# A first cross-attention that turns one unit of sixteen through TensorE, with small jobs moved off VectorE

## What is computed

```python
def _fq_unsigned(x, axis):
    s = jnp.max(x, axis=axis, keepdims=True) / 255.0
    s = jnp.maximum(s, 1e-08)
    q = jnp.clip(jnp.round(x / s), 0.0, 255.0) * s
    return x + jax.lax.stop_gradient(q - x)
...
q = _fq_sym(q, axis=-1)
k = _fq_sym(k, axis=-1)
v = _fq_sym(v, axis=2)
attn = jnp.einsum('bhqd,bhkd->bhqk', q, k)
attn = jax.nn.softmax(attn.astype(jnp.float32), axis=-1)
attn = _fq_unsigned(attn, axis=-1)
out = jnp.einsum('bhqk,bhkd->bhqd', attn, v)
...
x = _layernorm(x + _L0_xattn_ref(x, ctx_2048, ...), axis=-1)
```

## Time and profile before

| | |
|---|---|
| median of three runs | 3072.15 us |
| the profiled execution | 3072.58 us, span 3070.2 us |
| TensorE busy | 2597.4 us (85%) |
| VectorE busy | 1887.5 us (61%) |
| ScalarE busy | 1498.4 us (49%) |
| GpSimd busy | 449.3 us (15%) |
| the stage x0_attend | 984.1 (first scores) to 1693.1 us (last values) |
| transposes in it | 256, first start 990.6, last start 1687.9 us |

### The profile page before, as it was taken

How to read it: one execution, slowest core, us unless ns; L and a number is a source line. 1 busy time by engine, 2 the same in 40 slices (tenths; PEclk the granted TensorE clock), 3 DMA queues, 4 the chain that set the end, 5 groups by cost and what they waited for, 6 DMA issues and landing times. The chain is left out here.

```text
span 3070.2 us, 48513 instructions
## 1 busy us (share of the span) xinstructions
PE 2597.4 (85%) x16300; PEld 1616.7 (53%) x16470; DVE 1887.5 (61%) x3971; ACT 1498.4 (49%) x2696; POOL 449.3 (15%) x679
## 2 busy tenths in 40 slices
PE   4999999999975677767776797899868789999997
PEld 2777777777753233333333454555445545555554
DVE  5677777677757899999998112566546622323232
ACT  1555555555544688888887111566545511111110
POOL 1111111112110121222221000111122200000000
PEclk9999999999997788888877898999989989999999
DMA  4000000000001999999999000000022000000000
GB/s 178 1 1 0 0 0 0 0 0 0 0 25 34 198 198 196 198 195 197 197 198 198 24 0 23 1 0 0 0 72 76 18 1 1 0 0 0 0 0 27
DMA packets 566849, 173.12 MB, mean 56 GB/s; under 512 B 535445, under 2 KB 564945, under 8 KB 565713
## 3 DMA queue, kind: packets, MB, share of 16 engines
q1 hardware_dynamic: 562168, 163.91, 28.5%
q10 hardware_dynamic: 4568, 7.74, 0.7%
HBM read 35.29 MB, written 2.10 MB: 12 GB/s over the span
## 5 line engine op out<-in xcount | busy, mean ns | idle before, releaser
L1577 DVE TENSOR_SCALAR_CACHE_REDUCE x_row<-x_p_s,x_nsq 128x1024 f32<-128x1024 f32 x512 | 622.9, 1276 | 15.3 <-PE x_p_s L1395 15.3
L1457 ACT ACTIVATE x_ints<-x_row,x_nb 128x2048 uint16<-128x2048 f32 x256 | 511.6, 1999 | 111.2 <-DMA x_turned<-x_ints 70.2
L1395 PE MATMUL x_p_s<-x_kT,x_qz 128*128 128x512 bf16 x937 | 346.0, 457 | 163.9 <-DVE x_row L1577 151.4
L2384 DVE TENSOR_TENSOR f_h<-f_act_g,f_p_u 128x512 f32<-128x512 f32 (+1 forms) x132 | 90.7, 687 | 521.1 <-PE f_p_y L2277 451.3
L2327 ACT ACTIVATE f_act_g<-f_p_g 128x512 f32<-128x512 f32 (+1 forms) x132 | 78.4, 597 | 548.1 <-PE f_p_g L2262 548.1
L2262 PE MATMUL f_p_g<-f_xT,f_wg 128*128 128x512 f32 (+1 forms) x528 | 258.4, 613 | 16.8 <-ACT f_xT L2314 10.1
L2262 PE MATMUL f_p_u<-f_xT,f_wu 128*128 128x512 f32 (+1 forms) x528 | 252.4, 601 | 0.0
L2277 PE MATMUL f_p_y<-f_wd,f_h 128*128 128x256 f32 (+1 forms) x1056 | 247.5, 379 | 0.0
L2277 PEld LDWEIGHTS f_p_y<-f_wd,f_h 128*128 128x128 f32 (+1 forms) x1056 | 200.6, 190 | 77.2 <-issue 55.6
L1395 PEld LDWEIGHTS x_p_s<-x_kT,x_qz 128*128 128x128 bf16 x1024 | 72.5, 104 | 316.1 <-DVE x_row L1577 293.4
L1408 PEld LDWEIGHTS x_p_o<-x_vi,x_turned 128*128 128x128 f16 x4096 | 144.2, 100 | 144.4 <-DMA x_turned<-x_ints 80.1
(11 more groups left out here) (357 smaller groups left out, 4804.0 us busy)
## 6 DMA issues: line engine op xcount, KB each, us to landing
x_turned<-x_ints SPq DMA_TRANSPOSE x256, 4.8
f_wg<-in_L_ffn_w_dram SPq DMA_DIRECT2D x2, 1408.0 KB, 7.3
f_wu<-in_L_ffn_w_dram SPq DMA_DIRECT2D x2, 1408.0 KB, 7.1
f_wd<-in_L_ffn_w_dram SPq DMA_DIRECT2D x1, 2816.0 KB, 11.1
a_wq<-in_L_attn_Wq_dram SPq DMA_DIRECT2D x1, 2048.0 KB, 8.2
a_wk<-in_L_attn_Wlk_dram SPq DMA_DIRECT2D x1, 2048.0 KB, 17.4
a_wv<-in_L_attn_Wlv_dram ACTq DMA_DIRECT2D x1, 2048.0 KB, 17.9
a_wo<-in_L_attn_Wo_dram ACTq DMA_DIRECT2D x1, 2048.0 KB, 23.6
```

The source lines that it names most:

```text
L1395: mm = pe.matmul(p_s[n % SLOTS][:, c * BANK:(c + 1) * BANK], qz[b % 2][:, par, a, :], kT[:, a, at:at + BANK], start=True, stop=True)
L1457: act.activation(ints[k][:, :], rows[k][:, :, :].rearrange("p s n -> p (s n)"), ACT.Exp, bias=nb[:, k:k + 1], scale=-1.0, accum_out=esum[: ...
L1577: dve.tensor_scalar(rows[k][:, half, :], p_s[n % SLOTS][:, :], nsq[:, b % 2, h:h + 1], HIGHEST, ALU.mult, ALU.min, accum_out=(low if half ...
L2384: i = dve.tensor_tensor(h[n % 2][0:m, :], act_g[n % 2][0:m, :], p_u[n % 2][0:m, :], ALU.mult)
```

## The change

In each tile unit 2 (BY_ARRAY) is no longer turned by a transfer. TensorE turns its sixteen blocks of ints against the identity, eight at step 5 and eight at step 6, into the bank p_w, and ScalarE copies each eight to turned (ints_up, after exponentials 4 and 5). Semaphores t_made and t_read order the two, and turn_ints waits for its own unit's exponential and for p_w's former readers. SyncE skips the unit; the counts that wait for its transfers are recomputed by transfers(u).

The residual is no longer added by VectorE: TensorE adds core.x by a matmul with the identity into the projection's accumulation, and ScalarE copies the result to y. The scale, the negated scale and the epsilon of the variance go from VectorE to GpSimd. Jobs are put at other steps.

```diff
+    BY_ARRAY = 2
...
+        t_made, t_read = sem("t_made"), sem("t_read")
...
+        def by_array(u):
+            return u % PER_TILE == BY_ARRAY
+
+        def transfers(u):
+            return u // ROWS_KEPT + 1 - ((u - BY_ARRAY) // PER_TILE + 1 if u % ROWS_KEPT == BY_ARRAY else 0)
...
             for u in range(UNITS):
                 k = u % ROWS_KEPT
-                sp.wait_ge(e_up, u + 1)
-                after(sp, o_made, u - ROWS_KEPT + 1)
-                sp.dma_start(turned[k][:, :, :], ints[k][:, :], transpose=True).then_inc(t_in[k], 16)
+                if not by_array(u):
+                    sp.wait_ge(e_up, u + 1)
+                    after(sp, o_made, u - ROWS_KEPT + 1)
+                    sp.dma_start(turned[k][:, :, :], ints[k][:, :], transpose=True).then_inc(t_in[k], 16)
...
             def turn_reps(b):
                 pe.wait_ge(q_up, b + 1)
                 pe.wait_ge(rep_up, b + 1)
+                after(pe, t_read, 2 * b)
...
                 pe.matmul(p_w[:, 0:H], core.ones[:, :], core.bias("L0_xattn_bp"), start=True, stop=False)
+                pe.matmul(p_w[:, 0:H], core.ident[:, :], core.x[:, b, :], start=False, stop=False)
...
+            def turn_ints(half):
+                def run(b):
+                    u = b * PER_TILE + BY_ARRAY
+                    if half:
+                        pe.wait_ge(t_read, 2 * b + 1)
+                    else:
+                        pe.wait_ge(e_up, u + 1)
+                        if b + 1 < B:
+                            pe.wait_ge(q_up, b + 2)
+                        else:
+                            pe.wait_ge(y_up, b - 1)
+                    for c in range(B // 2):
+                        at = (half * B // 2 + c) * P
+                        mm = pe.transpose(p_w[:, :].bitcast(BF16)[:, c * P:(c + 1) * P], ints[u % ROWS_KEPT][:, at:at + P].bitcast(BF16),
+                                          core.identb[:, :])
+                    mm.then_inc(t_made, 1)
+                return run
...
-                pe.wait_ge(t_in[k], 16 * (u // ROWS_KEPT + 1))
+                if by_array(u):
+                    pe.wait_ge(t_read, 2 * (b + 1))
+                else:
+                    pe.wait_ge(t_in[k], 16 * transfers(u))
...
-                jobs(u, {1: [(turn_x, 1)], 3: [(project_q, 1)], 8: [(turn_reps, 1)], 11: [(turn_o, -1)], 13: [(project_o, -1)]})
+                jobs(u, {1: [(turn_x, 1)], 3: [(project_q, 1)], 5: [(turn_ints(0), 0)], 6: [(turn_ints(1), 0)],
+                         9: [(turn_reps, 1)], 12: [(turn_o, -1)], 14: [(project_o, -1)]})
...
+            def result_up(b):
+                act.wait_ge(y_made, b + 1)
+                after(act, x_up, b)
+                act.copy(y[:, :], p_w[:, 0:H]).then_inc(y_up, 1)
...
-                after(act, t_in[k], 16 * (u // ROWS_KEPT))
+                if by_array(u - ROWS_KEPT):
+                    after(act, t_made, 2 * ((u - ROWS_KEPT) // PER_TILE + 1))
+                elif u >= ROWS_KEPT:
+                    act.wait_ge(t_in[k], 16 * transfers(u - ROWS_KEPT))
...
+            def ints_up(half):
+                def run(b):
+                    u = b * PER_TILE + BY_ARRAY
+                    act.wait_ge(t_made, 2 * b + half + 1)
+                    after(act, o_made, u - ROWS_KEPT + 1)
+                    act.copy(turned[u % ROWS_KEPT][:, half * B // 2:(half + 1) * B // 2, :].rearrange("p k n -> p (k n)").bitcast(I32),
+                             p_w[:, :].bitcast(I32)).then_inc(t_read, 1)
+                return run
...
-                jobs(u, {1: [(query_up, 1)], 6: [(reps_up(0), 1)], 7: [(reps_up(1), 1)], 9: [(o_turned_up, -1)]})
+                jobs(u, {1: [(query_up, 1)], 4: [(ints_up(0), 0)], 5: [(ints_up(1), 0)], 7: [(reps_up(0), 1)], 8: [(reps_up(1), 1)], 10: [(o_turned_up, -1)], 13: [(result_up, -1)]})
...
+            def scales(b):
+                pool.wait_ge(amax_up, b + 1)
+                after(pool, rec_up, b)
+                pool.tensor_scalar(scl[:, :], amax[:, :], 1.0 / QMAX, FLOOR, ALU.mult, ALU.max).then_inc(scl_up, 1)
+
+            def negated(b):
+                pool.wait_ge(scl_up, b + 1)
+                after(pool, half_up, 2 * PER_TILE * (b - 1))
+                pool.tensor_scalar(nsq[:, b % 2, :], scl[:, :], -1.0, None, ALU.mult).then_inc(nsq_up, 1)
...
+            def variance(b):
+                pool.wait_ge(mean_up, b + 1)
+                pool.tensor_scalar(mv[:, 1:2], mv[:, 1:2], LN_EPS, None, ALU.add).then_inc(var_up, 1)
...
-                jobs(u, {4: [(integers, 1)], 5: [(scale_values, -1), (whole, 1)], 6: [(copies, 1)], 13: [(root, -1)], 14: [(norm, -1)]})
+                jobs(u, {3: [(scales, 1)], 4: [(negated, 1)], 5: [(scale_values, -1), (integers, 1)], 6: [(whole, 1)], 7: [(copies, 1)],
+                         15: [(variance, -1), (root, -1), (norm, -1)]})
...
-                jobs(u, {4: [(scale, 1), (denominators, -1)], 13: [(statistics, -1)], 14: [(variance, -1)]})
+                jobs(u, {4: [(denominators, -1)], 5: [(inverse, 1)], 15: [(statistics, -1)]})
                 if u < UNITS:
                     pass_over(u, 1)
-                jobs(u, {3: [(largest, 1)], 4: [(inverse, 1), (divided, -1)], 12: [(residual, -1)], 13: [(moments, -1)]})
+                jobs(u, {3: [(largest, 1)], 4: [(divided, -1)], 15: [(moments, -1)]})
```

More of the change, by code:

```diff
@@ L1511, in norm @@
                 pool.tensor_scalar(core.x[:, b, :], y[:, :], mv[:, 0:1], ln_r[:, 0:1], ALU.subtract, ALU.mult).then_inc(x_up, 1)
-            for piece in (integers, whole, copies):
+            for piece in (scales, negated, integers, whole, copies):
                 piece(0)
@@ L1528, in largest @@
                 dve.tensor_reduce(amax[:, :], heads(q[:, :]), AX.X, ALU.max, apply_absolute_value=True).then_inc(amax_up, 1)
-            def scale(b):
-                dve.wait_ge(amax_up, b + 1)
-                dve.tensor_scalar(scl[:, :], amax[:, :], 1.0 / QMAX, FLOOR, ALU.mult, ALU.max).then_inc(scl_up, 1)
             def inverse(b):
@@ L1537, in inverse @@
                 dve.reciprocal(rec[:, :], scl[:, :]).then_inc(rec_up, 1)
-                dve.tensor_scalar(nsq[:, b % 2, :], scl[:, :], -1.0, None, ALU.mult).then_inc(nsq_up, 1)
             def denominators(b):
@@ L1548, in divided @@
                 dve.tensor_tensor(heads(o_raw[:, :]), heads(p_o[:, 0:H]), bcast(rden[:, :], [P, XH, XD]), ALU.mult).then_inc(o_read, 1)
-            def residual(b):
-                dve.wait_ge(y_made, b + 1)
-                after(dve, x_up, b)
-                dve.tensor_tensor(y[:, :], p_w[:, 0:H], core.x[:, b, :], ALU.add).then_inc(y_up, 1)
             def statistics(b):
@@ L1562, in moments @@
                 dve.bn_aggr(mv[:, :], stats[:, :]).then_inc(mean_up, 1)
-            def variance(b):
-                dve.wait_ge(mean_up, b + 1)
-                dve.tensor_scalar(mv[:, 1:2], mv[:, 1:2], LN_EPS, None, ALU.add).then_inc(var_up, 1)
             def pass_over(u, half):
@@ L1586, in quantize_values @@
                     dve.tensor_scalar(vi[:, j * whole:(j + 1) * whole, :], vraw[j], ROUND, ROUND, ALU.add, ALU.subtract).then_inc(v_up, 1)
-            for piece in (largest, scale, inverse):
+            for piece in (largest, inverse):
                 piece(0)
```

## The result

| | before | changed |
|---|---|---|
| median (range), us | 3071.53 (3068.76 to 3073.97) | 3040.36 (3039.23 to 3045.75) |
| profiled execution, span | 3072.58, 3070.2 | 3045.75, 3043.9 |
| the stage: first VectorE pass to the last values | 985.2 to 1693.3: 708.1 | 986.8 to 1661.9: 675.1 |
| tile, mean of the thirteen from the third on | 42.89 | 40.67 |
| VectorE busy, and idle, in such a tile | 40.43, 2.46 | 39.88, 0.79 |

The ratio is 0.9902, 95% interval 0.9885 to 0.9919, against the forecast's 3044. Two later profiles of the same kernel have stages of 673.2 and 674.0 us and tiles of 40.57 and 40.55. The stage is 33.0 us shorter and the span only 26.3: outside the stage the two profiled executions differ by 6.7 us the other way (1.6 ahead of it, 5.1 behind it), in code that the change doesn't touch; that part varied between 2355 and 2369 us over the profiled runs here.

What follows compares the result with a forecast made beforehand. The transposes' queue bounds the stage at 42.9 us a tile; 40.2 + 0.7 = 40.9 after, so 15 × (42.9 − 40.9) = 30, less 1 at the end: 3072.6 − 29 = 3043.6 us. Range 3036 to 3056; 8 in 10, 3031 to 3063.

Steps and rivals of the forecast that it cites:

- Rival B: VectorE with its waits, not the queue, is the bound; only its 1.45 us a tile come off: 3052 us; chance 0.06.
- (1): Transfer queue: one transpose in sixteen goes, leaving 15 × 2.68 = 40.2 us a tile, 2.7 less.
- the interplay: ScalarE's late exponentials of units 5 to 9 reach an idle queue: 0.4 to 1.0 us a tile, 0.7 taken.
- "wrong" sign: Queue's cadence rising as transposes leave, its pauses set by time, not by count; gives back a part of (1).
- (2): VectorE loses residual sum, scale, negated scale and epsilon: 1.45 us less, its own tile time 39.8 us.
- (3): ScalarE gains three copies from PSUM, 1.55 us, 37.4 in sum: no bound, but exponentials at steps 4 to 8 fall late.
- (4): TensorE gains sixteen transposes and the identity matmul, 2.5 us, 33.5 in sum: no bound; step 6's wait mostly hidden.
- D: Slower: TensorE held at step 6 until exponential 4 and its copy finish; tile 43.9 us, 3089 us; chance 0.06.
- (5): GpSimd gains three operations of about 0.19 us and does epsilon, root and norm together at step 15: hidden.
- (6): First tile gives nothing, so 15 tiles count; behind the last transpose the last tile's chain costs 1 us more.
- A: The queue alone decides and the interplay costs nothing: 40.2 us a tile, 3033 us; chance 0.22.
- C: New in-order waits at step 6, slow projection and ScalarE's lateness all show: 42.3 us a tile, 3065 us; chance 0.18.

Runs made afterwards that it cites:

- the jobs alone: Changed kernel with no unit turned by TensorE, all 256 by transfers; only the residual, scale, negated scale and epsilon move off VectorE: 3072.45 us, ratio 1.0013.
- units 2 and 8: Changed kernel with unit 8 also turned by TensorE, former tile's result jobs a step later, statistics at next tile's step 0: 3046.43 us, ratio 0.9918.
- the turning alone: Changed kernel with VectorE's four jobs back on VectorE; only unit 2's turning through TensorE and ScalarE stays: 3046.56 us, ratio 0.9917.

## Why the prediction came out right, point by point

- **Bound.** Right. 15, 16 and 17 transfers give 40.67, 42.89 and 45.29 us a tile, and the jobs alone give nothing. The Trainium skill's 261 GB/s (DMA: Bandwidth & Descriptors, section "Latency and other measured facts"), by which the queue would have had room, is not reached by this form: 197 in the stage, and 210 even with nothing else running. Rival B is out with it.
- **(1) and the interplay.** The sum had 40.2 + 0.7 = 40.9; measured 40.67, 40.57 and 40.55. The loss of 0.4 to 0.5 was foreseen, but not its kind, and that the 0.7 came so near it is luck.

  I had put it to an idle queue at units 4 to 9. Such waits are there: in the thirteen tiles SyncE stood eight times at units 3 to 9 for an exponential or for TensorE's values, 4.1 us in all or 0.3 a tile, and 9.3 and 3.5 us in the two later profiles; elsewhere the transfers' rows stay 0.09 us apart, but for three pauses of 0.4. The longest one (1546.34 + 1.93 = 1548.27, and the next row starts at 1549.53; rows below) waited for the values.

  But the kernel without the turning has none of these waits and the same tile, 40.68 us. What both have is a longer beat: 15 × (2.71 − 2.68) = 0.45. That is what the prediction named as its "wrong" sign, pauses set by time and not by count, in a small dose. A part fits the instruction fetches: TensorE's weight loads, one to a matmul, grew from 342 in 42.9 us to 360 in 40.7, and a 16 KB fetch comes each 14.3 us for 15.6, which by 1.1 us each would be 0.26 us of a tile's 0.45. The kernel without the turning speaks against leaning on that: it has 344 loads a tile, 33 of these fetches from 1100 to 1600 us where the changed kernel has 35 and the one before 32, and the same beat of 2.71. How much of this step the fetches make, and what makes the rest, is open.

```profile
1546.34 1.93 SPq L1346 DMA_TRANSPOSE x_turned<-x_ints  x1
...
1549.53 2.10 SPq L1346 DMA_TRANSPOSE x_turned<-x_ints  x1
```

- **(2) VectorE.** Right to 0.05: its own tile is 39.75 (39.8 from 1.30 + 0.15). Two things hang on it: alone it is worth nothing, and without it the lost transfer gives 1.5 us a tile and not 2.2.
- **(3) ScalarE.** Two copies of 0.565 and one of 0.352 are 1.48 us for the 1.55; busy time rises by 0.85 (35.90 to 36.75), because rows overlap at their ends: only 1.20 of the copies lie outside other rows, and the exponentials' own part falls from 31.37 to 31.03. Its lateness costs nothing that shows: without the turning the time is the same.
- **(4) TensorE.** The wait is there in the predicted place. VectorE's waits for scores are 21.0 us in the whole stage, at the low end of the expected 20 to 40, but most of that is in the first two tiles; in the thirteen they are 5.3 us (before 1.1), in five places, four of them at step 7 and two of these over 1 us. The next rows, of the changed kernel's timeline, are one of them. The copy at 1219.54 follows exponential 4, which stands right behind one that waited 1.04 us for a landing; TensorE stands 1.12 us, and VectorE 0.40. In the other tiles VectorE's two passes in PSUM cover it, as D's "against" said. TensorE's busy time fell (30.98 to 30.00 us a tile) with 18 more matmuls a tile, sixteen turnings and two for the residual: the granted clock was 0.89 over the stage for 0.82.

```profile
1215.51 2.00 ACT L1501 ACTIVATE x_ints<-x_row,x_nb 128x2048 uint16<-128x2048 f32 x1 [1.04 <-DMA x_turned<-x_ints]
...
1217.54 2.00 ACT L1501 ACTIVATE x_ints<-x_row,x_nb 128x2048 uint16<-128x2048 f32 x1
...
1219.54 0.56 ACT L1509 COPY x_turned<-x_p_w 128x512 int32<-128x512 int32 x1
...
1220.16 1.04 PE L1426 MATMUL x_p_w<-identb,x_ints 128*128 128x128 bf16 x8 [1.12 <-ACT x_turned L1509]
...
1222.09 1.28 DVE L1631 TENSOR_SCALAR_CACHE_REDUCE x_row<-x_p_s,x_nsq 128x1024 f32<-128x1024 f32 x1 [0.40 <-PE x_p_s L1409]
```

- **(5) GpSimd.** The three operations took 0.44, 0.29 and 0.22 us and not 0.19 each: 0.95 us for 0.57. Hidden all the same. The statistics' wait is 2.9 us in all.
- **(6) First tile and tail.** By parts of the stage: tiles 0 and 1 gave 3.6 us, the thirteen 28.8, the last with its tail 0.6. At 2.2 for each of fifteen tiles, the first gave some 1.4 where I had nothing, and the tail cost about 1.6 for the 1: 15 × 2.2 + 1.4 − 1.6 = 33, where the sum had 29. The forecast tiles of 40.2 to 41.7 us, more alike than before, did not come: they run from 39.75, under the queue's mean, to 42.49.
- **Rivals.** A's 40.2 is not reached, for the longer beat. C and D did not happen, but with units 2 and 8 their mechanism appears and eats more than a transfer's gain.

## What to carry to other kernels

When a saturated queue and an engine stand within a few per cent (here 42.9 and 41.3 us a tile), price both floors: relief of one is capped by the other, and here two edits that took 24.6 us and nothing off the stage by themselves took 33.0 together. Count the queue's floor with the beat measured in the stage, and check it by adding a transfer as well as by leaving one out. In-order waits are free as long as the consumer has more work in hand than the producer is late, so put each such job away from where that producer is late already.

## What the runs showed of the hardware

- 128x2048 transposes of two-byte values between buffers on chip take 2.49 us each back to back with all engines idle (210 GB/s), and 2.66 to 2.71 in the stage.
- Instruction fetches share the 16 DMA engines with them: 16 KB for about 250 instructions of TensorE, about 1 us on one engine. Of 37 gaps over 3.25 us between landings of the kernel before, 36 hold such a packet; gaps without one have the median of the queue alone, 2.47 us. 192 more instructions a tile on GpSimd, which do nothing, brought 24 more packets of 8 KB in the stage, 64 bytes an instruction, and made the run 0.26% longer.
- TensorE's granted clock rose with more of its work in the same time. At one tile length (41.4 us), over 1100 to 1600 us, the turning alone (first row) against the kernel with one transfer left out (second row); one profile each:

```profile
1100.00:1600.00 500.00, 355.22 (x4245) 193.84 (x4316) 488.45 (x895) 442.12 (x472) 117.38 (x267) 0.92 1.12 191
```

```profile
1100.00:1600.00 500.00, 364.29 (x4072) 184.60 (x4136) 488.29 (x893) 432.05 (x448) 117.17 (x266) 0.86 1.11 191
```

The extra matmuls were thus paid back: 173 more of them in the stretch, and 9 us less of busy TensorE. Over the same stretch the changed kernel has 0.91, and 0.88 without its turning.
